# Grouped first stage and 64x64 tiles for the inverse's spectral product in an FNO tower

## The reference, cut to what matters

```python
h = einsum('bhwi,ic->bhwc', x, fc0_w) + fc0_b          # 3 -> 64 channels
for l in range(4):
    xf = rfft2(h)                                       # per image and channel
    top = einsum('bixy,ioxy->boxy', xf[:, :, :16, :16], w1)   # 16 + 16 rows, 16 columns of modes
    bot = einsum('bixy,ioxy->boxy', xf[:, :, -16:, :16], w2)
    sc = irfft2(top and bot in place, zero elsewhere)
    y = sc + einsum('bihw,oi->bohw', h, pw_w[l]) + pw_b[l]
    h = gelu((y - mean) * rsqrt(var + eps) * gamma + beta)    # mean, var over batch and pixels
out = gelu(h @ fc1_w + fc1_b) @ fc2_w + fc2_b
```

## Time and profile before

| | us |
|---|---|
| median of 3 runs | 4713.48 |
| lowest of them | 4712.67 |
| profiled execution | 4704.28 |
| its span in the profile | 4702.5 |
| TensorE busy | 3848.4 (82%) |
| VectorE busy | 2426.5 (52%) |
| ScalarE busy | 2074.1 (44%) |

### The profile page before, as it was taken

The page is one execution under the profiler, slowest core; times in us unless marked ns, Lnnn a source line. Parts: engine busy times, 40 slices in busy tenths (PEclk is TensorE's granted clock), DMA queues, the critical chain, the costliest instruction groups (busy, mean ns, idle before and its releaser), DMA issues. The chain is left out here.

```text
span 4702.5 us, 106559 instructions
## 1 busy us (share of the span) xinstructions
PE 3848.4 (82%) x46724; PEld 2478.1 (53%) x46724; DVE 2426.5 (52%) x3328; ACT 2074.1 (44%) x1708; POOL 29.0 (1%) x48
## 2 busy tenths in 40 slices
PE   5798998566989976669899766698998999568877
PEld 4495665344856653448566534485665222353432
DVE  1435555796345658953455588534554000364556
ACT  0022333552146655521566555215665999422322
POOL 0000000000000000000000000000000000100000
PEclk9898999788999998889999888898998999769788
DMA  1586887686789987767899877688998644002043
GB/s 36 241 310 178 210 212 208 254 301 239 306 318 365 365 298 268 294 246 306 314 365 363 299 263 288 253 308 310 364 365 293 211 167 165 11 1 64 10 88 67
DMA packets 217843, 1119.36 MB, mean 238 GB/s; under 512 B 24978, under 2 KB 96946, under 8 KB 139374
## 3 DMA queue, kind: packets, MB, share of 16 engines
q1 hardware_dynamic: 175438, 827.97, 49.4%
q10 hardware_dynamic: 41024, 285.23, 18.1%
q0 software_dynamic: 1024, 1.05, 0.1%
HBM read 709.04 MB, written 405.14 MB: 237 GB/s over the span
## 5 line engine op out<-in xcount | busy, mean ns | idle before, releaser
L523 PEld LDWEIGHTS bank<-fb,arena 64*128 64x128 f32 x8192 | 915.5, 307 | 230.0 <-issue 230.0
L523 PE MATMUL bank<-fb,arena 64*128 64x128 f32 x8192 | 963.3, 385 | 17.3 <-PE bank L501 12.3
L584 ACT ACTIVATE arena<-bank,pwb 128x1024 f32<-128x1024 f32 x512 | 542.5, 1111 | 677.4 <-PE bank L515 676.3
L628 DVE BATCH_NORM_STATS2 stats<-arena 128x6 f32<-128x512 f32 x1024 | 627.5, 674 | 159.3 <-ACT arena L584 159.3
L369 PE MATMUL bank<-arena 128*32 128x128 f32 x8192 | 588.9, 474 | 91.3 <-DMA arena<-in_w_modes 91.3
L620 DVE STREAM_TRANSPOSE arena<-bank 128x512 f32<-128x512 f32 x512 | 321.1, 684 | 614.1 <-PE bank L501 614.1
L765 ACT ACTIVATE arena<-arena,shift,scale 128x1024 f32<-128x1024 f32 x384 | 443.8, 1229 | 377.5 <-DMA arena<-y_dram 377.5
L725 PE MATMUL bank<-arena,fwq 32*32 32x512 f32 x6144 | 308.7, 822 | 355.2 <-DVE arena L770 355.2
L369 PEld LDWEIGHTS bank<-arena 128*32 128x32 f32 x8192 | 497.1, 134 | 183.0 <-issue 93.5
L576 ACT ACTIVATE arena<-arena,shift,scale 128x2048 f32<-128x2048 f32 x192 | 401.5, 2093 | 320.5 <-POOLq L167 167.5
L515 PE MATMUL bank<-arena,wst 64*64 64x512 f32 x4096 | 498.7, 602 | 0.0
(11 more groups left out here) (194 smaller groups left out, 2414.2 us busy)
## 6 DMA issues: line engine op xcount, KB each, us to landing
arena<-y_dram SPq DMA_DIRECT2D x224, 2048.0 KB, 9.9
y_dram<-arena ACTq DMA_DIRECT2D x256, 1024.0 KB, 11.8
arena<-spec_in SPq DMA_DIRECT2D x32, 2048.0 KB, 7.9
arena<-in_w_modes SPq DMA_DIRECT2D x32, 2048.0 KB, 14.2
spec_out<-arena SPq DMA_DIRECT2D x64, 1024.0 KB, 15.8
arena<-spec_out SPq DMA_DIRECT2D x112, 512.0 KB, 15.7
spec_in<-arena SPq DMA_DIRECT2D x24, 2048.0 KB, 13.6
spec_in<-arena ACTq DMA_DIRECT2D x4, 4096.0 KB, 11.7
```

What stands on the lines that cost most here:

```text
L523: mm = pe.matmul(hpx(bank[4 + T % 2 * 2 + i])[:, :, j * S:(j + 1) * S], a2[p % 2][CHAN[i]].rearrange("p v c r -> p (v c) r")[:, :, 4 * T + ...
L584: act.activation(hpx(yout[u])[:, :, T * BK:(T + 1) * BK], banks[:, 4 + T % 2 * 2:6 + T % 2 * 2, :], ACT.Identity, bias=pwb[:]).then_inc(y_ ...
L628: dve.bn_stats(stats[:, p * 48 + 6 * t:p * 48 + 6 * t + 6], hpx(yout[p % 2])[:, i, T * BK:(T + 1) * BK]).then_inc(y_seen, 1)
```

## The change

Two independent edits.

**First phase.** Loads are 8 (`NQ`) of 384 KB (four pairs each), all issued at the start, each with a buffer of its own. `rows0` does four pairs with 8 matmuls into two banks and one copy of 96x1024; `cols0` does four pairs with 4 matmuls by 256 columns (instead of 16 by 64) and one copy. Work on group i+1's rows is put ahead of group i's columns. The constant `c_f0` (now 97 rows of 512 numbers) is reordered so that `cols0` gives its result in four groups of 32 partitions (24 used), and `fc0` becomes 16 rounds of four matmuls of 32x128 by 512 columns in four row tiles. Each round fills four banks, two of which VectorE copies in one instruction, and two ScalarE. The fc0 bias row moves from a row of `v0` to a row of `z0`. TensorE waits only for `g0`, `c_f0` and the two `c_dc` rows; the other constants come on ScalarE's DMA queue. The stores to `spec_in` (4 MB each, as before) are issued by the sync engine, each block with a buffer of its own.

**Inverse.** `spectral` issues two 64x64 matmuls, one per output half v, where it issued one of 64x128; and each step's pointwise follows its own spectral.

```diff
-        x0 = [at(192 * u, 192) for u in range(2)]
+        x0 = [at(768 * i, 4, 192) for i in range(NQ)]
...
+            sp.dma_start(g0, d["c_g0"]).then_inc(basis_loaded, 16)
+            for i in range(NQ):
+                sp.dma_start(x0[i], d["x_rows"][4 * i:4 * i + 4].rearrange("q p x -> p q x")).then_inc(x0_loaded[i], 16)
+                if i == 0:
+                    sp.dma_start(f0c, d["c_f0"]).then_inc(basis_loaded, 16)
+                    for u in range(2):
+                        sp.dma_start(z0[u][96:97], ...).then_inc(basis_loaded, 16)
+            sp.dma_start(f0m, d["fc0_modes"]).then_inc(modes_loaded, 16)
+            for t in range(NB):
+                sp.wait_ge(fc0_first, 4 * t + 4)
+                sp.wait_ge(fc0_second, 4 * t + 4)
+                sp.dma_start(spec_in[...block t...], spec0[t]...).then_inc(spec0_stored, 16)
+            sp.wait_ge(spec0_stored, 16 * NB)
...
+            pe.wait_ge(basis_loaded, 16 * 4)
+            rows0(0)
+            for i in range(NQ):
+                if i + 1 < NQ:
+                    rows0(i + 1)
+                cols0(i)
+            pe.wait_ge(modes_loaded, 16)
+            pe.wait_ge(cols0_copied, NQ)
+            for t in range(NB):
+                for n in range(4):
+                    if t * 4 + n > 1:
+                        pe.wait_ge(fc0_first, t * 4 + n - 1)
+                        pe.wait_ge(fc0_second, t * 4 + n - 1)
+                    for g in range(4):
+                        rows_p = slice(32 * g, 32 * g + 32)
+                        mm = pe.matmul(bank[n % 2 * 4 + g][:], f0m[rows_p, n, :],
+                                       v0[rows_p, t * MB:(t + 1) * MB, :].rearrange("p b k -> p (b k)"),
+                                       start=True, stop=True, tile_position=(32 * g, 0))
+                        if g % 2 == 1:
+                            mm.then_inc(fc0_done, 1)
...
                 for j in range(4):
                     for i in range(2):
-                        mm = pe.matmul(hpx(bank[4 + T % 2 * 2 + i])[:, :, j * S:(j + 1) * S],
-                                       a2[p % 2][CHAN[i]].rearrange("p v c r -> p (v c) r")[:, :, 4 * T + j], hpx(fb2[CHAN[i], :]),
-                                       start=(j == 0), stop=False, tile_position=(i * C, 0))
+                        for v in range(2):
+                            mm = pe.matmul(hpx(bank[4 + T % 2 * 2 + i][CHAN[v], :])[:, :, j * S:(j + 1) * S],
+                                           a2[p % 2][CHAN[i], v, :, 4 * T + j], hpx(fb2[CHAN[i], :]),
+                                           start=(j == 0), stop=False, tile_position=(i * C, v * C))
...
-                for T in (2 * e, 2 * e + 1):
-                    pe.wait_ge(y_copied, n * 4 + (T + 1))
-                    spectral(p, T)
-                if not first:
-                    pe.wait_ge(h_ready, n * 2 + (e + 1))
-                for T in (2 * e, 2 * e + 1):
-                    pointwise(p, T).then_inc(y_done, 1)
+                pe.wait_ge(y_copied, n * 4 + (T + 1))
+                spectral(p, T)
+                if T % 2 == 0 and not first:
+                    pe.wait_ge(h_ready, n * 2 + (T // 2 + 1))
+                pointwise(p, T).then_inc(y_done, 1)
...
+                for T in range(4):
+                    if T % 2 == 0 and p < NP - 1:
+                        rows(p + 1, (T // 2,))
+                    columns(p, T)
```

More of the change, by code:

```diff
@@ L85, in tower_layout @@
     out["pw_t"] = np.ascontiguousarray(pw_w.transpose(0, 2, 1))
-    f = np.zeros((6 * M2 + 1, M2, 2, C), np.float32)
+    f = np.zeros((4, 32, 4, 2, C), np.float32)
     for ri in range(2):
         for j in range(3):
[L90 to L93, removed]
+            for k in range(4):
+                f[:, k * 6 + ri * 3 + j, k, ri] = fc0_w[j]
+    f[0, 24, 0, 0] = fc0_b
+    out["fc0_modes"] = f.reshape(P, 4, P)
     out["fc0_t"] = np.ascontiguousarray(fc0_w.T)
@@ L188, in build @@
-        assert 1024 + B * K1 + M2 * P + 512 <= 8192
-        def sync_spectrum0(sp):
[L191 to L213, removed]
@@ new lines, in tensor_spectrum0, with rows0, cols0 @@
+        def tensor_spectrum0(pe):
+            def rows0(i):
+                pe.wait_ge(x0_loaded[i], 16)
+                if i > 1:
+                    pe.wait_ge(rows0_copied, i - 1)
+                for q in range(4):
+                    for wh in range(2):
+                        col = q % 2 * 256 + wh * P
+                        mm = pe.matmul(bank[i % 2 * 2 + q // 2][0:96, col:col + P], x0[i][:, q, wh * 96:(wh + 1) * 96], g0,
+                                       start=True, stop=True)
+                mm.then_inc(rows0_done, 1)
+            def cols0(i):
+                pe.wait_ge(rows0_copied, i + 1)
+                if i > 1:
+                    pe.wait_ge(cols0_copied, i - 1)
+                for k in range(4):
+                    part, wh = k // 2, k % 2
+                    col = wh * P + part * 2 * K1
+                    mm = pe.matmul(bank[4 + i % 2][:, 0:256], f0c[:, part * 2 + wh, :], z0[i % 2][:, :, col:col + 2 * K1],
+                                   start=(k == 0), stop=(k == 3))
+                mm.then_inc(cols0_done, 1)
+            pe.wait_ge(basis_loaded, 16 * 4)
[18 more added lines that the diff above has]
+                            mm.then_inc(fc0_done, 1)
@@ L219, in tensor_spectrum0 @@
             pe.wait_ge(const_loaded, N_CONST)
+            pe.wait_ge(fc0_first, 4 * NB)
+            pe.wait_ge(fc0_second, 4 * NB)
             pe.matmul(bank[0][:, 0:P], fc0t[:], pw[:], start=True, stop=True)
             pe.matmul(bank[1][:, 0:1], pw[:], fc0b[:], start=True, stop=True).then_inc(pw0_done, 1)
[L223 to L241, removed]
@@ L276, in build @@
[L276 to L285 removed]
+        N_CONST = 16 * (5 + 2 + 10 + 3)
```

125 lines of the change are left out of this document (66 added, 59 removed).

## The result

The changed kernel takes 4486.95 us (median of 4 runs, 4476.43 to 4495.51), the kernel before 4714.27 in the same session: a ratio of 0.952, 95% interval 0.949 to 0.954. The forecast was 4400 in a range of 4300 to 4540. So the change is faster, by 227 us instead of 314.

A forecast was written before the change was run, and what follows sets the result against it. It took latency to bound the first phase and TensorE the inverse, with DMA nearly full in layers 1 to 3. 4704.3 - 112 - 107 - 90 = 4395, plus half of the median's 9 us excess, gave 4400 us, range 4300 to 4540.

The forecast's parts named there:

- First phase: Start to first barrier: TensorE starts at 12 us, stores at 410 GB/s end the phase at 96 instead of 208: -112 us.
- The spectral round: Inverse on TensorE: a round of four 64x64 tiles takes 0.115 us, a half pair 4.4, a pair 8.9.
- 0.165: Rival in the inverse: a tile's weight load and stream run in turn, 10.4 us a pair at least, 4435 us; chance 0.10.
- 0.219: Rival in the inverse: twice the records at an unchanged round time, so the tiles change nothing, 4587 us; chance 0.11.
- 0.287 us a round: Rival in the inverse: four tiles cost what L369's cost, a half pair 7.17 us instead of 6.43, 4781 us; chance 0.06.
- no effect: Rival in the inverse: the tiles change nothing, only the remainders and the first phase's gain are won, 4587 us; chance 0.11.
- Layer 0: Layer 0's inverse: TensorE, VectorE and DMA at 8 to 9 us give 9.4 a pair, -107 us, bounds -123 and -58.
- my DMA term: Layer 0's inverse: stores, modes and x at the 312 GB/s of a store stretch take 8.7 us a pair.
- Layers 1 to 3: Their inverses: DMA nearly full, 12.0 us a pair, -30 a layer, -90 in all, bounds -10 and -150.
- DMA already at its ceiling: Rival in layers 1 to 3: TensorE's time becomes waiting, 4704 - 112 - 107 - 10 = 4475 us; chance 0.21.
- The reordering: Inverse: moving each pointwise behind its own spectral costs nothing.
- Forward, mix, head, tail unchanged: The phases that the change doesn't touch: unchanged to a few us.

The follow-up runs named there:

- hin4: The changed kernel with a fourth input buffer and one set of semaphores for both kinds of load: 4460 us, ratio 0.945.
- resident: hin4 with TensorE's inverse as a hardware loop of 4 pairs, GpSimd copying each pair's modes into one of four fixed blocks: 4443 us, ratio 0.944.
- twoq: The changed kernel with the lower half's output store moved to the sync queue: 4469 us, ratio 0.949.
- whole: resident with each pair's output stored by one transfer from all 128 partitions, values from layer 1 on not the reference's: 4321 us, ratio 0.916.
- shift: The kernel before with two GpSimd memsets added at the end of the first phase: 4716 us, ratio 1.000.
- p1_only: The kernel before with only the first phase's edit, the inverse as before: 4654 us, ratio 0.987.
- tiles_only: The changed kernel with its 64x64 tiles in the old order, both spectral products and then both pointwise: 4586 us, ratio 0.970.
- order_only: The changed kernel with the spectral product back in 64x128 matmuls, each pointwise still behind its own spectral: 4693 us, ratio 0.995.

## Why the prediction was right or wrong

**First phase: right, in size too, with a little luck.** -112 forecast, -112 measured. The start was 15.7 us instead of 12; the pair loop then took 30 us instead of 36, as from the second group on each took 3.5 us, where I had counted 7 for the first two; so two errors cancelled, and the stores began at 53 us instead of 54. The step that sets the end, four stores at 410 GB/s, was the right one.

**The spectral round: right.** 0.114 us for 0.115, and 4.4 us a half pair. The rivals with 0.165, 0.219 and 0.287 us a round fell. L1143's row, the same tile and length, was the one to go by; L369's wasn't. The rival "no effect" had a slip of its own: the two remainders are 0.7 us a pair, 22 us in layer 0, where its sum takes 5.

**Layer 0: the step that failed.** "I take 9.4 for what they cost each other" and "-107"; measured 11.6 and -49, outside even the far bound of that term (11 us, -58). My three parties (TensorE 8.9, VectorE 8.0, DMA 8.7) lacked a fourth, the instructions themselves: smaller tiles raise TensorE's matmuls and weight loads from 224 to 352 a pair (2 x 3588 and 2 x 5636 over 32, and the window of after). A packet holds some 252 of them (352 x 200 / 11.63 over 24 packets), so it is used up in 8.3 us instead of 14.4. That was 1.8 to 2.1 us a pair (after 11.63, hin4 11.92, resident 9.83), 36 us of the phase against after and 47 against hin4 in the profiled executions, shown by resident; the medians give 17 to 46 for the whole kernel. The rest was my DMA term: 8.7 us from 312 GB/s in one slice of 5 us (the slice behind it reads 129), where resident sustains 268 at full share over 200 us, and a pair takes 9.83. I had read five microseconds as the rate, and didn't know that a store from 64 partitions alone moves at little more than half the rate of both halves together (twoq: 219 and 395 GB/s). Of instructions the Trainium skill, "Runtime: NRT & Kernel Launch", section Instruction fetch mechanics, says that the sequencer fetches them by its own DMA in blocks of 16 KiB, 256 each, and that the cost of crossing a block is mostly hidden; the trace agrees with the size, and hidden it was before the change (no gap of that kind in 200 us), not after it (27 us in 200). With both taken away (whole) the inverse is 329, 120 less than before: TensorE's 8.9 a pair was right, and is reached.

**Layers 1 to 3: right.** 12.0 us a pair and -30 each forecast; 12.0 to 12.4 and -28, -26, -25. The rival "DMA already at its ceiling" has the right bound at the wrong height: DMA sets the pair, but 387 GB/s pass where 365 did before. whole, with 379 to 395 and 24 us less a layer, shows that even that wasn't the ceiling. The Trainium skill's limit of about 358 GB/s for a core to HBM ("DMA: Bandwidth & Descriptors", Specifications), by which nothing was to be won here, is passed by after's 387 over 300 us, and the measurement decides.

**The reordering: wrong, small.** "Costs nothing" proved a gain of some 13 us an inverse with the new tiles; by what wait I can't say, as the steady pairs of layer 1 are nearly equal (12.17 against 11.63 us in layer 0, but 12.38 against 12.03 in layer 1).

**Forward, mix, head, tail unchanged: right** for after, but for 12 us in the forward phases, which unchanged code shows as well (shift). The terms in sum: forecast -112 - 107 - 90 = -309; measured -112 - 49 - 79 + 12 = -228. The total of 4487 lies inside the range, but nearest to the rival "DMA already at its ceiling" (4475), whose mechanism it isn't: that rival gives layer 0 107 us and layers 1 to 3 together 10, and they gave 49 and 79.

## What to carry to other kernels

Before cutting matmuls into smaller tiles, count instructions as a resource: so many per pair against the 250 or so that a packet holds here, and look at the "instruction" queue and at waits named "issue" where nothing is waited for; a loop that stays resident, even at the price of a copy on an idle engine, gives the time back. Take a DMA ceiling from a long stretch of the same access, not from one short slice, and store from all 128 partitions at once where the layout allows it. A part tested alone can lose its gain in a phase that it doesn't touch: compare phase by phase.

## What the runs showed of the hardware that I had not expected

- TensorE stands still in straight code when its instructions come late: 10 gaps, 27 us of 200, at 352 matmuls and weight loads in 11.6 us, with DMA 87% busy. A loop of 92 KB ran with one instruction packet in 200 us, one of 185 KB with as many as straight code. Whether the packet is asked for late or waits behind data isn't shown.
- How many partitions are stored at once set the rate: 8 KB packets from 64 partitions alone took 0.55 to 0.57 us in twoq (219 GB/s at a share of 0.94), and 0.33 to 0.36 us with the other 64 partitions stored beside them from a second queue (395 GB/s); one store from 128 partitions with 16 KB packets took 0.325 per 8 KB.
- Identical forward phases took from 316 to 357 us, with the granted clock between 0.85 and 0.78, by kernel: p1_only and tiles_only were slow in all three of theirs (338 to 357), no other profile in any (up to 328). What in those two kernels does it stays open.
- Four more changes a pair between 64x128 and 64x64 tiles went with 0.85 us more, 0.21 us each (order_only; each pointwise also stands at another place in the order there).
